# Linear attention with a routed network on one core: each batch's shared network moves into the batch's own attention step, and two wide subtractions move from GpSimd to VectorE

## The reference

```python
xn = (x - mean) / sqrt(var + 1e-5)                      # x: 16 batches, 512 tokens, 256 wide, float32
Q = elu(xn @ Wq.T + bq) + 1;  K = elu(xn @ Wk.T + bk) + 1;  V = xn @ Wv.T + bv
KV = einsum('bnd,bne->bde', K, V);  Z = einsum('bnd,bd->bn', Q, K.sum(1) + 1e-6)
attn = (einsum('bnd,bde->bne', Q, KV) / Z[..., None]) @ Wo.T + bo
combine = route(xn, gate_weight)                        # 16 experts, 4 groups, best 2 groups, best 4 experts, x 2.5
moe = sum over experts of combine * (silu(xn @ up[e]) @ down[e])     # up 256x128, down 128x256
shared = silu(xn @ shared_up) @ shared_down             # 512 hidden units
out = x + attn + moe + shared
```

## Time and profile before

| what | us |
|---|---|
| median of 3 runs (lowest, highest) | 947.47 (947.15, 953.37) |
| the profiled execution's own time | 947.18 |
| its span in the profile | 945.4 |
| busy: PE, DVE, ACT, POOL | 773.7, 736.0, 552.2, 639.9 |
| first stage, to the end of the last batch's routing | 0 to 526 |
| last shared network and plan, to `plan_ready` | 526 to 545 |
| second stage | 545 to 945 |

### The profile page before, as it was taken

One profiled execution on the slowest core, in us unless ns is written; L12 is line 12 of the kernel. 1 busy time (PEld: TensorE's weight loads), 2 busy tenths in 40 slices (PEclk: granted clock), 3 DMA queues, 4 the chain that ended last, 5 costly groups with the idle time before them and its releaser, 6 DMA issues.

```text
span 945.4 us, 19895 instructions
## 1 busy us (share of the span) xinstructions
PE 773.7 (82%) x5264; PEld 696.7 (74%) x5264; DVE 736.0 (78%) x2499; ACT 552.2 (58%) x1141; POOL 639.9 (68%) x613
## 2 busy tenths in 40 slices
PE   3469888988899889988898679888887888889860
PEld 2469777977788778878898678777776777778750
DVE  5568788888978898889888858777777877778760
ACT  3436645665556555665555257666676776667640
POOL 2117766876677667777787757777777777777771
PEclk9779999999999999999999979999999999999995
DMA  4121543454335433533233389999999999999999
GB/s 132 42 83 73 173 175 105 154 179 173 122 134 183 169 120 136 185 125 131 85 115 108 134 285 350 319 334 327 317 354 305 330 339 322 321 308 359 325 322 300
DMA packets 142317, 202.16 MB, mean 214 GB/s; under 512 B 16176, under 2 KB 117184, under 8 KB 142208
## 3 DMA queue, kind: packets, MB, share of 16 engines
q1 hardware_dynamic: 114144, 116.47, 39.3%
q0 software_dynamic: 28064, 84.43, 23.5%
HBM read 104.19 MB, written 105.04 MB: 221 GB/s over the span
## 4 chain that ended last, share of the span: by engine, by line
DVE 32%; DMA 24%; PE 13%; issue 12%; POOL 8%; ACT 6%; SPq 2%; DVEq 1%; POOLq 0%; ACTq 0%
DMA x_in<-rows_by_expert 7%; DMA rows_by_expert<-xn,f_id 6%; PE bank_a L310 5%; DMA rows_by_expert<-xn,slots_now 5%; DMA xn<-rows_by_expert 5%; POOL rows_by_expert L487 4%; DVE xn L1139 3%; DVE xn L1173 3%; PE bank_x L310 3%; POOL rows_by_expert L524 2%; PE bank_a L1358 2%; DVE so_far L912 2%; DVE hs_l L1184 2%; DVE xt_l L777 2%; DVE chain L926 2%
## 5 line engine op out<-in xcount | busy, mean ns | idle before, releaser
L524 POOL DMA_INDIRECT rows_by_expert<-xn,f_id x286 | 277.5, 970 | 94.8 <-issue 68.3
L478 POOL DMA_INDIRECT rows_by_expert<-xn,slots_now x192 | 192.4, 1002 | 55.0 <-issue 55.0
L657 ACT CAST xt_h<-bank_a 128x512 fp32r<-128x512 f32 x143 | 83.9, 586 | 68.0 <-PE bank_a L1358 62.7
L1161 DVE TENSOR_TENSOR xt_l<-bank_a,xt_h 128x512 fp32r<-128x512 f32 x143 | 98.2, 687 | 26.1 <-ACT xt_h L657 25.6
L487 POOL DMA_INDIRECT rows_by_expert<-xn,slots_now x64 | 72.7, 1136 | 67.0 <-DVE xn L1146 48.8
L569 ACT ACTIVATE hid<-bank_x 128x512 f32<-128x512 f32 x64 | 37.8, 591 | 118.3 <-PE bank_x L310 118.2
L310 PE MATMUL bank_y<-ws,hs_h 128*128 128x256 f32 x512 | 97.7, 288 | 4.4 <-DVE hs_l L945 4.4
L310 PE MATMUL bank_x<-xt_h,ws 128*128 128x512 f32 x256 | 90.8, 396 | 0.0
L310 PEld LDWEIGHTS bank_y<-ws,hs_h 128*128 128x128 f32 x512 | 82.7, 193 | 8.1 <-DVE hs_l L945 5.2
L677 ACT ACTIVATE hid<-bank_x 128x256 f32<-128x256 f32 x143 | 54.8, 383 | 41.2 <-PE bank_x L310 37.4
L310 PE MATMUL bank_y<-ws,hs_l 128*128 128x256 f32 x256 | 73.3, 286 | 0.0
(11 more groups left out here) (278 smaller groups left out, 2548.3 us busy)
## 6 DMA issues: line engine op xcount, KB each, us to landing
xn<-rows_by_expert SPq DMA_DIRECT2D x215, 272.0 KB, 4.5
x_in<-rows_by_expert SPq DMA_DIRECT2D x71, 272.0 KB
rows_by_expert<-spare SPq DMA_DIRECT2D x22, 544.0 KB, 5.5
x_in<-in_L_attn_x_dram SPq DMA_DIRECT2D x16, 512.0 KB, 7.3
out_dram<-rows_by_expert SPq DMA_DIRECT2D x8, 1024.0 KB, 14.1
rows_by_expert<-xn,f_id POOLq DMA_INDIRECT x286
rows_by_expert<-xn,slots_now POOLq DMA_INDIRECT x256, 2.6
w_raw<-in_L_ffn_expert_up_dram SPq DMA_DIRECT2D x32, 64.0 KB, 1.9
```

What stands on the lines that cost most here:

```text
L478: G.indirect_dma_start(out=half_rows[:, :], in_=xn[:, c % NB, s, 0:RW], in_offset=None, out_offset=bass.IndirectOffsetOnAxis(ap=slots_now[ ...
L524: G.indirect_dma_start(out=half_rows[:, :], in_=f_y[u % YB][:, tile], in_offset=None, out_offset=bass.IndirectOffsetOnAxis(ap=f_id[:, u % ...
L657: S_.copy(f_h[u % 4], A[u % 2][:, :].rearrange("p (c s t) -> p c s t", c=KD, s=2)).then_inc(fx_hi, 1)
L1161: V.tensor_tensor(f_l[u % 4], A[u % 2][:, :].rearrange("p (c s t) -> p c s t", c=KD, s=2), f_h[u % 4].bitcast(F32), ALU.subtract).then_inc ...
```

## The change

The loop runs over c = 0 to 15. Step 0 has no shared network, as before. Step 1 does batch 0's chunks where it did them before, and behind its own attention all four chunks of batch 1 in a row. From step 2 on each step does its own batch's shared network, at the same places in the order. The sum of `bank_y` into `xn` (now `shared_sum`) moves: from the end of a step, behind `route_chain`, to the next step, behind `route_scores`. The 17th step goes; its plan stands behind the loop, without a shared network between its parts, and the last batch's `shared_sum` behind the plan. `xr_l` and `q_l` are made on VectorE (`rows_split` behind the two `q_f` instructions, `queries_split` ahead of `route_groups`). GpSimd keeps the scatters and the small power function.

```diff
+        def first_chunk(c):
+            return 0 if c == 1 else SH * c
...
-            for c in range(B + 1):
-                if c < B:
-                    pool.wait_ge(xr_hi, c + 1)
-                    G.tensor_tensor(xr_l[:, :, :], xn[:, c % NB, :, 0:D], xr_h[:, :, :].bitcast(F32), ALU.subtract
-                                    ).then_inc(xr_lo, 1)
+            for c in range(B):
                 if c >= 2:
-                    scatter_first(c - 2)
+                    scatter_first(c - 1)
                 if c + 1 < B:
                     inverse_root(c + 1)
                 if c >= 1:
-                    scatter_rows(c - 1, 0, 3 if c < B else REST)
-                if c < B:
-                    pool.wait_ge(q_hi, c + 1)
-                    G.tensor_tensor(q_l[:, :, :], q_f[:, :, :], q_h[:, :, :].bitcast(F32), ALU.subtract
-                                    ).then_inc(q_lo, 1)
-                    if c >= 1:
-                        scatter_rows(c - 1, 3, REST)
+                    scatter_rows(c - 1)
+                if c == 1:
+                    scatter_first(0)
...
+            scatter_rows(B - 1)
             scatter_first(B - 1)
...
+            def rows_split(c):
+                dve.wait_ge(xr_hi, c + 1)
+                V.tensor_tensor(xr_l[:, :, :], xn[:, c % NB, :, 0:D], xr_h[:, :, :].bitcast(F32), ALU.subtract
+                                ).then_inc(xr_lo, 1)
+
+            def queries_split(c):
+                dve.wait_ge(q_hi, c + 1)
+                V.tensor_tensor(q_l[:, :, :], q_f[:, :, :], q_h[:, :, :].bitcast(F32), ALU.subtract
+                                ).then_inc(q_lo, 1)
+
+            def shared_sum(c):
+                dve.wait_ge(down_done, SH * (c + 1))
+                base = xn[:, c % NB, :, RW:RW + D]
+                V.tensor_tensor(base, Y[:, :, :].rearrange("p a (s d) -> p (a s) d", d=D), base, ALU.add
+                                ).then_inc(y_summed, 1)
...
+                route_scores()
+                if c >= 2:
+                    shared_sum(c - 1)
...
+                rows_split(c)
+                route_group_scores()
...
+                queries_split(c)
+                route_groups()
...
+                if c == 1:
+                    shared_sum(0)
+                    hidden_low(SH)
+                    hidden_low(SH + 1)
+                    set_shape(5)
+                    hidden_low(SH + 2)
+                    hidden_low(SH + 3)
+                    set_low(5)
+
+            count_units()
+            plan_units()
+            plan_rows()
...
+            shared_sum(B - 1)
+            set_low(SH + E - 1)
...
+                if c == 1:
+                    up(SH, 1)
+                    pe.wait_ge(rank_read, c + 1)
+                    for m in range(SH, 2 * SH):
+                        if m + 1 < 2 * SH:
+                            up(m + 1, 1)
+                        down(m)
+                if with_shared and after:
+                    up(SH * (c + 1), (c + 1) % 2)
```

More of the change, by code:

```diff
@@ L472, in inverse_root, with scatter_rows @@
                 G.tensor_tensor(rstd[:, c % 2], var_eps[:, :], minus_half[:, :], ALU.pow).then_inc(var_done, 1)
[L474 removed]
+            def scatter_rows(c):
                 pool.wait_ge(route_ready, c + 1)
[L476 removed]
+                for n in range(SUB * (TOP_K - 1)):
                     s, k = n // (TOP_K - 1), 1 + n % (TOP_K - 1)
@@ new lines, in _ @@
+                warm(ACT.Exp)
+                wait(act, k_lo, c)
+                wait(act, den_ready, c)
+                if c == 0:
+                    act.wait_ge(turned, 2)
+                for s in range(SUB):
+                    act.wait_ge(k_done, SUB * c + s + 1)
+                    S_.activation(k_f[:, s, :], A[s][:, 0:D], ACT.Exp, bias=minus_one[:, 0:1])
+                    S_.activation(r_exp[:, s, :], A[s][:, D:KG], ACT.Exp, scale=-1.0).then_inc(k_exp, 1)
+                if c == 0:
+                    set_high(1)
@@ new lines, in _ @@
+                act.wait_ge(k_ready, SUB * (c + 1))
+                wait(act, p_done, KD * c)
+                S_.copy(k_h[:, :, :], k_f[:, :, :]).then_inc(k_hi, 1)
+                if with_shared:
+                    hidden_high(n)
+                else:
+                    act.wait_ge(folded, 1)
+                    S_.copy(wvo_h[:, :, 0:D], Y[:, 0, :].rearrange("p (c d) -> p c d", c=KD)).then_inc(folded_hi, 1)
+                wait(act, q_lo, c)
+                for h in range(KD):
+                    act.wait_ge(q_done, KD * c + h + 1)
+                    S_.activation(q_f[:, h, :], A[h][:, :], ACT.Exp, bias=minus_one[:, 0:1]).then_inc(q_exp, 1)
@@ new lines, in _ @@
+                route_chain(c)
+                if after:
+                    set_low(c + 3 if c < 2 else c + 4)
+                if c == 1:
[9 more added lines that the diff above has]
+            plan_rows()
+            dve.wait_ge(plan_turned, 1)
@@ new lines, in _ @@
+            V.tensor_copy(table, A[0][0:COLS, 0:UR].rearrange("p (j u) -> p j u", j=2))
+            plan(V.tensor_tensor(experts_f, A[1][0:1, 0:WORDS * PACK].rearrange("p (w k) -> p w k", k=PACK),
+                                 place[:, :].unsqueeze(1).to_broadcast([1, WORDS, PACK]), ALU.mult))
+            planned()
+            plan(V.tensor_reduce(packed_f, experts_f, AX_X, ALU.add))
+            planned()
+            V.tensor_copy(packed, packed_f).then_inc(plan_ready, 1)
+            shared_sum(B - 1)
@@ L1281, in _ @@
                     down(n)
[L1282 to L1291 removed]
+                pe.wait_ge(k_lo, c + 1)
+                pe.wait_ge(xr_lo, c + 1)
+                for h in range(KD):
+                    cols = slice(h * P, (h + 1) * P)
+                    last = split3(A[2][:, h * D:(h + 1) * D],
+                                  [(xr_h[:, s, cols], xr_l[:, s, cols], k_h[:, s, :], k_l[:, s, :])
+                                   for s in range(SUB)])
+                last.then_inc(m_done, 1)
+                if with_shared:
                     up(n + 2, par)
@@ L1347, in _ @@
-                if before_ and now:
-                    down(n + 3)
-                    up(n + SH, c % 2)
-            pe.wait_ge(y_summed, B)
+                pe.wait_ge(m_lo, c + 1)
+                if c == 0:
+                    pe.wait_ge(folded_lo, 1)
+                    pe.wait_ge(eps_ready, 1)
+                    pe.wait_ge(consts_cast, 1)
+                for h in range(KD):
+                    cols = slice(h * P, (h + 1) * P)
+                    T_.matmul(A[2 + h][:, 0:PW], ones_wide[:, :], eps_rows[:, :], start=True, stop=False)
+                    split3(A[2 + h][:, 0:PW],
+                           [(m_h[:, d, cols], m_l[:, d, cols], wvo_h[:, d, :], wvo_l[:, d, :])
+                            for d in range(KD)], start=False).then_inc(p_done, 1)
@@ new lines, in _ @@
+                for s in range(SUB):
+                    last = T_.matmul(X[1][:, (s + 1) * E:(SUB + 1) * E].rearrange("p (s e) -> p s e", e=E),
+                                     ones_wide[:, :],
+                                     mask_r[:, s, :].unsqueeze(1).to_broadcast([P, SUB - s, E]),
+                                     start=False, stop=s == SUB - 1, skip_group_check=True)
+                last.then_inc(rank_done, 1)
+                if with_shared:
+                    down(n + 2)
@@ new lines, in _ @@
+                pe.wait_ge(p_lo, KD * (c + 1))
+                pe.wait_ge(q_lo, c + 1)
+                for s in range(SUB):
+                    if s >= 2 and after:
+                        pe.wait_ge(xt_lo, KD * (c + 1) + s - 1)
+                    cols = slice(s * P, (s + 1) * P)
+                    split3(A[(s + 2) % SUB][:, 0:PW],
+                           [(q_h[:, d, cols], q_l[:, d, cols], p_h[:, d, :], p_l[:, d, :])
+                            for d in range(KD)]).then_inc(c_done, 1)
```

329 lines of the change are left out of this document (114 added, 215 removed).

## The result

| | before | after |
|---|---|---|
| median of 14 runs each (lowest, highest) | 947.48 (945.30, 953.37) | 955.57 (953.72, 958.57) |
| ratio, 95% interval | | 1.0081 [1.0067, 1.0095] |
| the profiled execution, its span | 947.18, 945.4 | 953.72, 952.0 |

The change made the kernel 0.8% slower: within 1%, but further than the spread of the runs, which do not overlap. The forecast was 948.0, with a range of 933 to 960.

What follows compares the result with a forecast made beforehand. It took a TensorE-VectorE ring, delayed by VectorE standing still for GpSimd, as the bound. Step 1 +12.7, middle steps -2.9, step 15 -2.7 and behind the loop -6.3 gave +0.8 on 947.18: 948 us, range 933 to 960.

Steps and rivals of the forecast that it cites:

- The standing still: Between attention output and `k_f`, VectorE loses about 2.9 us a step to GpSimd's `xr_l`; moving the subtraction removes it.
- The rival in which VectorE goes on standing still: Another cause than `xr_l` keeps 2.9 us at each step's end; 968 us, chance 0.08.
- a second price: In the old loop, idle time ahead of `q` halves the clock in 12 of 14 steps, costing `q` 1.47 us.
- The ring of the middle step: Middle steps, TensorE and VectorE: `m` waits 2.7 us for `xr_l`, starting at t = 12.25; 29.65 us at full clock.
- The clock: Middle steps: falls in 12 of 14 at 1.35 us each, so 30.8 a step; -2.9 us over 13 steps.
- the clock rival: Falls become rare behind the wait ahead of `m`; 29.65 us a step, 933 us; chance 0.23 for 931 to 941.
- The bound of 31.1: Upper bound for a middle step, with one fall of the clock in each step at 1.47 us.
- the forecast's own case: New wait ahead of `m` with clock falls in most steps; 943 to 955 us, chance 0.52.
- the rival with a longer wait: Falls in each step plus a second wait at `p` or `down`; 31.5 to 31.8 a step, 955 to 962, chance 0.17.
- Step 1: Batch 1's whole network adds 11.3 us and waits of about 1.7 and 0.8; +12.7 us, bounds +11 and +16.
- step 15: No statistics of a next batch, so `m` starts at t = 10.3 instead of 13.0; -2.7 us, bounds -1 and -4.
- behind the loop: From last routing to `plan_ready`, work leaves and the second stage starts earlier; -6.3 us, bounds -4 and -7.

Runs made afterwards that it cites:

- h3_network_only: Changed kernel with both subtractions (`xr_l`, `q_l`) back on GpSimd at their old places; 964.43 against 947.28 for the kernel before, ratio 1.0179.
- the filler: Changed kernel with 11 unused matmuls a step ahead of `m` from step 2 on; 937.79 against 950.28 for the kernel before, ratio 0.9874.
- splits: Kernel before with only `xr_l` and `q_l` moved to VectorE, at the changed kernel's places; 940.04 against 947.28, ratio 0.9913.

## Why the prediction was right and where it was not

**The standing still, and the cure.** Right. With the subtractions off GpSimd the 3 us instructions are gone at the seam, and none has come up elsewhere. The rival in which VectorE goes on standing still has fallen, and h3_network_only shows the cause from the other side: with the subtractions back on GpSimd they are back, two a step. The Trainium skill, page "SBUF — State Buffer", section "Who interferes with whom", says that such a pair locks one another out for the whole instruction. These rows agree as to who waits and until when: `we` ended at 268.97 and `xr_l` at 268.40, `hs_l` at 285.99 and `q_l` at 285.43, so the loss is GpSimd's 2.40 and 0.2 to 0.5 us more. The rows also have VectorE's instruction beginning 0.3 to 0.6 us ahead of GpSimd's each time, and still ending behind it.

**What bounded the old step.** Here the prediction was wrong, without harm to its sum. It said that "a step is a ring through TensorE and VectorE" and that the wait ahead of `q` has "a second price", the slow clock. But in 10 of the 13 steps from 98 on, the chain that ended last has no TensorE instruction at all; the two steps of the earlier trace rows are among the three that do. Pieces of the chain from one sum to the next, before the change:

```profile
283.69 1.14 DVE xn L1146
...
288.17 1.75 POOL rows_by_expert L487
...
290.22 4.52 DMA rows_by_expert<-xn,slots_now
...
297.90 1.08 ACT xn L541 x2
...
309.80 3.03 DVE masked L915
...
314.82 1.14 DVE xn L1146
```

It goes from the sum through the scatters and their landing to ScalarE's normalisation (the wait for old scatters, of which the prediction said "TensorE is not held by it"), then through VectorE to the instruction that stands still, and to the next sum. Timeline of GpSimd over the same step:

```profile
285.60 0.99 POOL L487 DMA_INDIRECT rows_by_expert<-xn,slots_now  x1 [4.08 <-DVE xn L1146]
...
291.70 1.04 POOL L472 TENSOR_TENSOR rstd<-var_eps,minus_half 128x4 f32<-128x4 f32 x1 [0.52 <-DVE var_eps L729]
...
309.34 0.96 POOL L478 DMA_INDIRECT rows_by_expert<-xn,slots_now  x1 [0.30 <-issue]
310.32 2.40 POOL L498 TENSOR_TENSOR xr_l<-xn,xr_h 128x1024 fp32r<-128x1024 f32 x1
316.74 0.98 POOL L487 DMA_INDIRECT rows_by_expert<-xn,slots_now  x1 [4.01 <-DVE xn L1146]
```

`xr_l`, which sets the end of the standing still, starts when GpSimd's list has come to it, in every step, and from the sum to its end, 27.1 us, GpSimd waits for others only 0.5. So the old step was GpSimd's 27.1 and VectorE's 4.0 behind it (27.1 to 27.9 and 2.9 to 4.1 over the steps); TensorE's wait came of that. The clock bears it out: the two steps without a fall, from `q` at 222.92 and at 254.13, took 31.21 and 31.67 us, the eleven with one 30.3 to 31.6. The forecast survived because it took the old step as measured, and because it added up the new one from TensorE's and VectorE's rows, where TensorE really is in the ring: there GpSimd waits 7.5 to 8.8 us a step for the sum in steps 4 to 14, and TensorE's part of the chain that ended last is 33% of the span, against 13% before. That the mistake did no harm is in part luck: the same reading went into the expectation for the network alone, and there it missed by 26 us.

**The ring of the middle step.** Right in kind and in its main number. Forecast: no wait ahead of `q`, 2.7 us ahead of `m`, `m` at t = 12.25, 29.65 a step at full clock. Measured: 2.67 to 2.74 in steps 2 to 14; `m` of step 9 at 336.85, behind a silu at 324.68, so t = 12.2; 29.85 in the two steps without a fall and 29.86 with the filler.

**The clock: the term that was mis-sized.** The prediction said "falls in 12 of 14 steps, as now", at 1.35 each, for 30.8 a step. Falls were as frequent, 11 of 13, and the clock rival's 933 did not come. But a single one cost 1.44 in the mean (1.2 to 1.5), and two of the 11 were double, at 2.7. Over 13 steps that is 406.35 - 13 x 29.85 = 18.3 us for the clock, where 15.1 were allowed; the ring without falls, 0.2 a step too short, makes up another 2.6. Together these are the 6 us by which the sum is off (+6.6 against +0.8). The bound of 31.1, "a fall in each step, at 1.47", was no bound, since a step can lose twice that: the period was 31.26. The measured 955.6 lies past the forecast's own case (943 to 955), in the band of the rival with a longer wait (955 to 962); but that rival's second wait at `p` or `down` did not come, and the mechanism was the forecast's.

**Step 1, step 15, behind the loop.** +12.1 against +12.7, -2.3 against -2.7, -6.3 against -6.3. The waits in step 1 were 1.60 and 0.64, forecast 1.7 and 0.8. Within the last term two errors cancel: `plan_ready` came 13.9 behind the last routing and not 12.6, and the second stage took 1.3 less than before. That the last routing "stays near 528" contradicted the prediction's own terms, which add up to 533; it came at 538.8.

**What the parts are worth.** The prediction netted the two parts of the change against each other and never priced them apart. Apart they are -7 (splits) and +17 (network), which would be +10 if they simply added; together they are +8. The network's move costs 14 us up to seam 2 and 0.4 to 0.7 us in each further step, and gives back 5 to 7.5 behind the last routing (the table of the four parts). In short: the 17th step was cheap, because its network ran beside the plan. Why the network's move alone shortened no middle step, the rows of GpSimd say: with the subtractions there, its list fills the ring in both kernels.

**The point that the prediction walked past.** It had the idle time ahead of `k_f` in its hands ("about 1.6 to spare") and `xr_l` as what holds `m`, and did not put them together. The one instruction of 1.22 us, moved there, is worth 44 us (911.4 against 955.6, on different chips of the first kind; the ratios are 0.9609 and 1.0081).

## What to carry to other kernels

Before you move a wide VectorE or GpSimd instruction, ask not only whether its engine has room but who waits for it at the new place: the same subtraction costs a wait of 2.7 us a step behind `q_f` and nothing ahead of `k_f`, 955.6 against 911.4. Where TensorE is in the ring, a wait of that length costs more than itself, since the clock can fall behind it, at times twice; filling it with useless matmuls gave back 1.3 us a step. Where TensorE was not in the ring, as in the kernel before, the fall cost nothing that can be seen: so follow the chain through many steps, not through one, before you name what bounds a loop. An engine's busy share does not tell it either: GpSimd was busy 22.4 of 31 us and still waited for others only 0.5 us between the sum and the end of `xr_l`. And an idle stretch can be a shelter: taking it away exposed GpSimd's other subtraction. Compare on more than one chip before you call a gain of a few per cent a property of the kernel.

## What the hardware showed that was not expected

Behind waits of one length (2.67 to 2.74 us) with the same work around them, the granted clock fell in 11 of 13 steps, in two of them with twice the loss of the others, and not at all in two.

GpSimd's indirect transfer takes 0.96 us to issue, but 1.61 where VectorE's `k_l_p` subtraction runs (271.91 to 273.06 beside the row at 272.30 in h3_network_only), in each step; in the kernel before the same pair gives 1.75 to 1.77. So the interference seems to reach the scatters too; no run moves the subtraction away to show it.

On two groups of chips the same kernel took 947 to 950 and 1121 to 1139 us. On the slower ones groups of matmuls were released up to three times as far apart as TensorE's rows say, and there the edit that gains 3.9% on the others loses 1.2%.
